# A four-layer transformer kernel on one core: room of its own for raw weights, a spread in four transfers, blocks of products of ones, and a new order

## What is computed

```python
x = x + 0.5 * L0_ffn(layernorm(x))      # gate, up, down; 704 hidden; weights (wq - 128) * scale; silu
x = x + L0_attn(layernorm(x))           # 16 heads of 16, causal, rope
x = x + 0.5 * L0_ffn(layernorm(x))
x = x + 0.5 * L1_ffn(layernorm(x))      # weights quantised to -1, 0, 1 by their mean magnitude, sigmoid
x = x + L1_attn(layernorm(x))           # 16 query heads on 4 key heads, causal, alibi, output bias
x = x + 0.5 * L1_ffn(layernorm(x))
```

## Time and profile before

| what | value |
|---|---|
| median of three runs | 583.99 us (583.89 to 584.03) |
| span of the profiled execution | 584.2 us |
| busy in that span | PE 535.6, DVE 461.8, ACT 401.5, POOL 340.4 us |
| mean granted clock of TensorE | 0.984 of full |

### The profile page before, as it was taken

The page is one execution under the profiler, slowest core; times in us unless marked ns, Lnnn a source line. Parts: engine busy times, 40 slices in busy tenths (PEclk is TensorE's granted clock), DMA queues, the critical chain, the costliest instruction groups (busy, mean ns, idle before and its releaser), DMA issues.

```text
span 584.2 us, 12653 instructions
## 1 busy us (share of the span) xinstructions
PE 535.6 (92%) x4924; PEld 290.7 (50%) x4924; DVE 461.8 (79%) x813; ACT 401.5 (69%) x605; POOL 340.4 (58%) x427
## 2 busy tenths in 40 slices
PE   2887987998999999999899998999999999999987
PEld 1353642544653654655546564465455644553664
DVE  4888979898889789589986878887897767783454
ACT  5866576678577758855687756867769596669433
POOL 2367886864896578844645167624455724437543
PEclk9978997999999999999999999999999999999999
DMA  8700020121022100310210102010211021001301
GB/s 327 311 2 1 22 88 1 55 74 42 20 85 65 37 4 3 121 65 1 77 40 3 47 17 74 22 41 0 69 41 38 4 78 50 22 1 41 111 0 73
DMA packets 19627, 31.73 MB, mean 54 GB/s; under 512 B 6464, under 2 KB 7872, under 8 KB 19416
## 3 DMA queue, kind: packets, MB, share of 16 engines
q1 hardware_dynamic: 19568, 30.93, 15.0%
HBM read 13.75 MB, written 2.36 MB: 28 GB/s over the span
## 4 chain that ended last, share of the span: by engine, by line
PE 57%; DVE 14%; ACT 9%; POOL 7%; issue 7%; DMA 5%; SPq 1%; DVEq 0%; POOLq 0%; ACTq 0%
PE PS L583 17%; PE PS L607 10%; PE PS L694 9%; PE PS L674 4%; DVE MX L1050 4%; PE PS L625 4%; PE PS L659 4%; PE PS L567 3%; ACT PB L838 3%; PE PS L709 3%; DMA RB<-scratch 2%; ACT XN L761 2%; PE PS L539 1%; DVE MX L1046 1%; DVE ST L863 1%
## 5 line engine op out<-in xcount | busy, mean ns | idle before, releaser
L838 ACT ACTIVATE PB<-PS 128x1024 f32<-128x1024 f32 x160 | 158.9, 1024 | 50.3 <-PE PS L674 43.2
L1050 DVE TENSOR_REDUCE MX<-PS 128x2 f16<-128x1024 f32 (+2 forms) x192 | 158.4, 865 | 23.1 <-PE PS L539 22.9
L583 PE MATMUL PS<-XT,WGU 128*128 128x512 f16 x660 | 158.2, 382 | 2.8 <-DVE PB L990 1.1
L1126 POOL TENSOR_TENSOR HH<-TH,HH 128x512 f16<-128x512 f32 x71 | 82.2, 1168 | 86.1 <-ACT HH L806 85.8
L1154 POOL TENSOR_SCALAR_AFFINE_SELECT PB<-PB 128x512 f32<-128x512 f32 (+1 forms) x140 | 73.2, 550 | 53.1 <-ACT PB L838 53.1
L583 PEld LDWEIGHTS PS<-XT,WGU 128*128 128x128 f16 x660 | 59.1, 98 | 74.1 <-issue 5.9
L607 PE MATMUL PS<-WD,HH 128*128 128x256 f16 x660 | 78.0, 273 | 1.1 <-POOL HH L1126 0.6
L694 PE MATMUL PS<-PB,V 128*32 128x512 f32 (+3 forms) x1024 | 75.5, 435 | 1.3 <-POOL PB L1154 1.1
L607 PEld LDWEIGHTS PS<-WD,HH 128*128 128x128 f16 x660 | 62.4, 98 | 14.0 <-issue 3.1
L659 PE MATMUL PS<-SK,SQ 63*128 63x256 f16 (+3 forms) x512 | 60.7, 300 | 6.5 <-DVE MX L1050 3.6
L674 PE MATMUL PS<-SQ,SK 64*128 64x384 f16 (+3 forms) x512 | 58.5, 300 | 8.0 <-ACT PB L838 2.4
(11 more groups left out here) (122 smaller groups left out, 756.4 us busy)
## 6 DMA issues: line engine op xcount, KB each, us to landing
SQ<-QPB SPq DMA_DIRECT2D x24, 256.0 KB, 2.5
OC<-OT SPq DMA_DIRECT2D x16, 256.0 KB, 2.4
RB<-scratch SPq DMA_DIRECT2D x32, 128.0 KB
SK<-QPB SPq DMA_DIRECT2D x12, 256.0 KB, 3.1
SQ<-MT SPq DMA_DIRECT2D x128, 1.0 KB
out<-X SPq DMA_DIRECT2D x8, 256.0 KB, 2.2
PB<-gu SPq DMA_DIRECT2D x2, 704.0 KB, 6.1
X<-x_in SPq DMA_DIRECT2D x2, 512.0 KB, 5.4
```

The lines of the kernel that those rows point to most:

```text
L583: m = e.matmul(o[:, :], WGU[l][:, k, col:col + P], rows_of(f)[j][:, k, :], start=j == 0 and k == 0, stop=j == 1 and k == 1)
L838: e.activation(PB[Q % 2][:, j, :, :], two_banks("s", i), ACT.Exp, scale=0.25).then_inc(a_exp, 1)
L1050: e.tensor_reduce(mx[:, :, pr, t], o[:, :, col:col + (t + 1) * P], AX.X, ALU.max, negate=True).then_inc(a_max, 1)
L1126: e.tensor_tensor(hh[1][:, s * T:(s + 1) * T], value_of(j)[0], hh[0][:, s * T:(s + 1) * T], ALU.subtract).then_inc(f_lo, 1)
```

## The change

Raw weights get a tile of their own, `LATE`, and ACT's late `k` letters wait for nothing but the masks' semaphore. `R` issues four transfers, one for each group of 32 neighbouring partitions, each with 16 as its outermost number of repeats; the semaphore rises by 64. A new PE letter `z` runs eight products of ones (128x128 by 256 columns, 16 bits) into a PSUM bank that nobody reads, after a wait for `ONE`. The new string has 17 of them: ten ahead of the first `t`, then one, two, two, one and one, all before the first `m`. The batches' rows, rotation table and masks are loaded ahead of the raw weights of layer 1. POOL sets its three constants first. All strings and banks are written anew; apart from `z`, each engine has the same letters as before, the same number of each. The scratch room for software transfers is set to 256 bytes; the kernel has no such transfer.

```diff
 ORDER = {
     "sp":
-        "kkrrkrkrDSrRDSRrkrDSRkrrDSRrrDrkSRkDSRrrlkkrDrSRrDSlRrkrkDrSRrDSrRrkkrDrSRDrSRrDkrkSRDrSRrrrDSRDOSOR"
-        "OOOOOO",
+        "kkrkrrkDrSrRDSRrrkDSkRrrDSRrrDrkSlRkDSRrrkkrrDSRrlDSRrkkrrDSrDRSrRrkkrDSrDrSRRrDrkkSRDrSRrOOrrDSRDSR"
+        "OOOOOO",
     "pe":
-        "ttggGggGaGgttGGggGggddddGaGgtggGuutGqqddddvqgGgvgqGGGgugugGqttqmmgmgmmmmmqmsqsdsmgGmsdmsdmmsdsmmpmsG"
+        "zzzzzzzzzzttzgggGGgGGggttzzaGggggGdddgdzzGGtatzgGGuuqqqddddvqgggggGGGGvuugGttqqzmmmggmmmmmqmsqssdmgG"
...
     "dve":
-        "NwNtthwwhwkhwhwhtwthwwNhhwwdwNdwhnhwhkuuhtpqptqdwdpqhnpqhhkuuhhhpqttqpmmmmmxmmmspqsmhpmqxhmdmsmmdmxm"
+        "NwNtthNhhkhwwwttwhhwwhhwwdNdwwwnhhwwhuukphptwqqdtppdhnqqhhhhkuuhttpqpqmmmmmmxmmssmqqpphmxhmdmmmsmxmd"
...
     "act":
-        "TwwXxxwttthXtthxxhhwhtwhkttwwwthwhXtkhwxthYwyyhthXxkQQvtkthQtvYQtyytthhxxhhQTkQkktthkeeeteeQeeQhhoee"
+        "TwwXxxwtwthkttXtthxxhhkkhhtttkwwwhthXktXYyyxhhxthhvQQttthkttwYvyQyQtxxhhhhwThkktQQteweeewteeQeQhhoee"
...
     "pool":
-        "wrwwrhhhhwhwrdhdrewhhhhsasqdadsqaesaqqhwshsahahqqhfsafsdfafqdhqfffffhefhffcfhCffhcCssaaqqfffrssadaqq"
+        "wwwrrrhhhhhdhdrewwhhhhssadaqqdsesaaqqhssaawhhhhqqssfaafwfdqfqdffhhfefffffhcfffhhCcCssaaqfffrsqadsaqq"
...
-ONE_BANK, TWO_BANKS, SHARED = "tgGuqvoapd", "ms", "do"
+ONE_BANK, TWO_BANKS, SHARED = "tgGuqvoapdz", "ms", "do"
...
+        LATE = sb("LATE", [P, 2, 4 * T])
...
-        late = [t[1][:, :, :].rearrange("p h t -> p (h t)").bitcast(F32) for t in (SQ, SK)]
+        late = [LATE[:, k, :] for k in range(2)]
...
+        ONES = ONE.bitcast(BF16)
...
             e.dma_start(BO[:, :], bo1).then_inc(l_a0, 16)
+            e.dma_start(X[:, 2 * NT:, :], x_in[:, 2 * NT:, :]).then_inc(l_x23, 16)
+            e.dma_start(ROPE[:, :, :], rope).then_inc(l_c2, 16)
+            e.dma_start(MASKW[:, :, :, :], maskw).then_inc(l_c2, 16)
+            e.dma_start(MASKM[:, :, :, :], maskm).then_inc(l_c2, 16)
             e.dma_start(rd[0], wd1[:, 0:4, :]).then_inc(l_w3, 16)
             e.dma_start(rd[1], wd1[:, 4:, :]).then_inc(l_w3, 16)
             for k in range(2):
                 e.dma_start(rgu[k], gu1[:, k, :]).then_inc(l_w1, 16)
-            e.dma_start(X[:, 2 * NT:, :], x_in[:, 2 * NT:, :]).then_inc(l_x23, 16)
-            e.dma_start(ROPE[:, :, :], rope).then_inc(l_c2, 16)
-            e.dma_start(MASKW[:, :, :, :], maskw).then_inc(l_c2, 16)
-            e.dma_start(MASKM[:, :, :, :], maskm).then_inc(l_c2, 16)
...
-                    w.wait_ge(t_si[u], 32 * (n - 1))
+                    w.wait_ge(t_si[u], 64 * (n - 1))
...
-                    for g in range(2):
-                        e.dma_start(RB[g:P:2, u, :], src[:, g, :].unsqueeze(1).to_broadcast([4, 16, T])).then_inc(t_si[u], 16)
+                    for a in range(4):
+                        e.dma_start(RB[32 * a:32 * a + 32, u, :], src[a].unsqueeze(0).to_broadcast([16, 2, T])).then_inc(t_si[u], 16)
...
-                if c == "a":
+                if c == "z":
+                    w.wait_ge(p_pool, 3)
+                    wait_bank(w, "z", i)
+                    o = bank("z", i)
+                    for _ in range(8):
+                        e.matmul(o[:, 0:256], ONES[:, 0:P], ONES, start=True, stop=True)
+                elif c == "a":
...
                     w.wait_ge(l_c2, 48)
-                    if z == 1:
-                        w.wait_ge(p_dve, 30)
...
-                    w.wait_ge(t_si[u], 32 * (n + 1))
+                    w.wait_ge(t_si[u], 64 * (n + 1))
...
-    nc = bacc.Bacc("TRN2", target_bir_lowering=False, num_devices=1)
+    nc = bacc.Bacc("TRN2", target_bir_lowering=False, num_devices=1, dynamic_dma_scratch_size=256)
```

More of the change, by code:

```diff
@@ new lines @@
+        "smdsmmdsmdsmmpmssGmsgsGmsspmssgmmGmmpsmsmsgssGmmmpmssvsvmsmsuummmpqqssoooomssddsqqmmmpttdsssdgmsggsG"
+        "GggmpmmsGsmssmmgsGGmmpssmmvvuussddmmddsmqqspmottosoossgsmqgmggmGGGsgmspsmmgssGqtGtpssgdsssdddpggGgGm"
+        "mgvgmmmvGuuGGmmooomoqmsqmssqmsmdsmddmdmssmmspmsmssmmsttspgssmgGGgggmmsGGgGmsspmsttddddssmggpmmmvgggu"
+        "uGsGGssqmqsmgGsmqGssoompmmddddmssomsommpmttsssggssGGsgmmmpsgGmssgmmGGgmpsmsvsmsmmmdddmsdsspssmttoomm"
+        "gggsGuuooqqqGsmmsgmGGsggGsmpmmsdmmsddsmsdmsspsmsmsmmspttvsmmggggGGGGggGsmmssttssddddoooommpsmpuugsmm"
@@ new lines @@
+        "qqssqsggsGGssspmsmgGmmpmmvgmmmGgmssGsmststmmpddddssmoomgssoomsggmGGmsmpmsgsssGggssspssttGGpggGgddddG"
+        "GgggGGooooddddttgGggGgGgGGgdddd",
+    "dve":
+        "NwNtthNhhkhwwwttwhhwwhhwwdNdwwwnhhwwhuukphptwqqdtppdhnqqhhhhkuuhttpqpqmmmmmmxmmssmqqpphmxhmdmmmsmxmd"
+        "mkhmsnmhmxmsmmhmmmcsxhmmmmcmmuxummmppxqqooNdmqppmmmqttdcmsxhsshhnkmsmmmhmmxsshhmmmmxcuudmmdNppmqqmtt"
+        "ooNmxmhpmhqkhmhmmxhqptthcsdhdknsshchmssmmmmhuuxshmmhoommlmlxmmmdlmdmmxNmmmmmxttNmhhkchmmhhhmmxttddnm"
+        "shsmmmskcsuuhxhhmlmssmlhhlommxmddmNmmmoxmttNhhmmchkmmhmxhmhmmmcxmmmmddnmxttmmosssuuhokhlllhmmmshssxh"
+        "hmmmmcmdxmdmNmmmmNxttmmchhkhhhhmmttddxnoomNmmuuhmmxlllckhhmmhmmmxmmmmmchhmxmttdmdmomhxoNmmhhmmmxkhch"
+        "httchhddhkhhhooNXttddhhhkhhhdd",
@@ new lines @@
+    "act":
+        "TwwXxxwtwthkttXtthxxhhkkhhtttkwwwhthXktXYyyxhhxthhvQQttthkttwYvyQyQtxxhhhhwThkktQQteweeewteeQeQhhoee"
+        "eteheeoeetYoeeeteehhhoeeevveeyycceoeeQeeQXoxxQeeeQtetthehhtoeeeettheYhhoevevcyyeeceeXoxxeQeetettXQhh"
+        "ehtteeoheetxxQhheoeeeetQhottthhtvtYvcyyhchheQQeeeQeeeeoeeXexxeeoteethhtttheXthhheeoxxeeettYcovhttyye"
+        "heeQhhteteQcQeehheeeoXoxxeeetteeethhoetheetXthhhoeeveeceeecoeexxYttteyyhQQQeehhtetthehhoeeeeeeoeeeXe"
+        "oxxvettXhththhttheeheexxcceYeooyytXeQQeeeQthteeeeohhetovttheeeeehhoxxcceeteeetthXhehoeeeteteeeeetoxx"
+        "hhhotctthhhtctthhhXxxttthhhtthhth",
@@ L139 @@
+        "frffhffhhhhccCCeffhhfhhhfffddfffrrhhchchhffCCbefrfffffhfhbhhhccCCffrfhhffffffhhchChchChhhrhhhhh",
     "banks":
[L140 to L143, removed]
@@ L144 @@
[L144 to L146 removed]
+        "3722733416563147324563743511241352071653540260761313765406145146726450134763462014242642612652402606"
+        "2560260426046250426050264205624064025264026520650304620126401624716240210426153204612476201652702640"
@@ new lines @@
+        "6206246102642046324602740246012564216026502470636201624604621460362530467204257024520764620572351624"
+        "5620436402460364704206205604206247620740264563206423416420643212064213460253472506720526027520430624"
+        "3641264024660360246054027647240725426056241043046304620461244272406730462705431043604261470246724162"
+        "4146202642460620462065401264137543601370246032640167420641245026452064270456024602546056024260456205"
+        "62046520727204740621463206720462416420672046043210607521503274167416342731672414571",
```

20 lines of the change are left out of this document (1 added, 19 removed).

## The result

| kernel | median | runs | against before |
|---|---|---|---|
| before | 583.94 us | 582.37 to 584.03 (4) | |
| after | 575.83 us | 573.70 to 576.52 (4) | 0.9855 [0.9835, 0.9875] |

The change is 8.1 us faster, where I had forecast 3.0 (581.0; the range 575.5 to 585.5 holds it). Its profiled execution has a span of 574.1 us and a mean granted clock of 0.988, beside 584.2 and 0.984 before. The two profiles are not quite a fair pair. Of the 10.1 us between the two spans some 2 belong to that one execution. A line number of the changed kernel lies eight to ten above that of the same statement before.

What follows compares the result with a forecast made beforehand. DVE was taken to bound the first 101.7 us, with PE busy for nearly all the rest. Terms of -1.0, -0.5, -0.5 and -1.0 summed to -3.0 us: forecast 581.0 us, range 575.5 to 585.5.

Steps and rivals of the forecast that it cites:

- E: Spread in four transfers: each lands 1.5 us sooner; -1.0 us in all, range -2.0 to +1.1.
- B: First 40 us in the new order: PE gains a lead but DVE bounds the stage; -1.0 us, between -3.3 and +1.7.
- D: Own room for raw weights: ACT's last four fills no longer wait for quantising; -0.5 us, range 0 to -2.1.
- A: Ten blocks ahead of the first rows: end at 13.8 us, first unit 1.3 us late but at 2.4 GHz.
- C: Seven other blocks: hidden by PE's wait for DVE, returning lower-clock time; -0.5 us taken.
- F: New order past 101.7 us: 19.6 us of holes can shrink or grow, -2 to +2; 0 taken.
- rival "slower": Ahead of the first turns: blocks overrun, ending at up to 19.8 us; price up to 5, 586 us; chance 0.15.
- fewer than three stretches at the lower level: Sign for PE's clock: lower-level stretches number fewer than three after 16 us.
- a DMA share well above 0.25: Sign for the spread: RB's transfers show this share and POOL's waits are shorter by 1.5 us each.
- rival "nothing": PE's lead waits for DVE and PE's other work hides the spread: 583.0 to 585.0 us; chance 0.12.
- check on row maxima: Sign at the first stage's end: row maxima from about 86 us instead of 88.2.
- check on idle time past 101.7: Sign that the forecast is wrong: idle time past 101.7 us over 21 us.

Runs made afterwards that it cites:

- e8: Kernel before with four transfers for a spread and nothing else new: 582.10 us, 0.9962.
- e7: New strings without blocks of ones up to the first row maxima, old strings behind, with the change's loads and room: 580.74 us, 0.9934.
- e3: Changed kernel with new strings, blocks included, up to the first row maxima and the old strings from there on: 583.45 us, 0.9993.
- e10: Changed kernel whose strings switch to the old ones at the end of the third attention, about 260 us: 581.23 us, 0.9954.
- e13: Changed kernel with old strings only from the first row maxima to 260 us, new front with 17 blocks and new order behind: 578.79 us, 0.9900.
- e5: Changed kernel without the ten blocks of ones ahead of the first rows, the other seven kept: 572.10 us, 0.9787.
- e6: Changed kernel with the ten blocks ahead of the first rows and none of the other seven: 572.01 us, 0.9791.
- e2: Changed kernel without any of its 17 blocks of ones, orders and banks else unchanged: 571.86 us, 0.981.
- e14: Changed kernel with POOL's two late w letters moved early and the first ten blocks alone: 571.01 us, 0.9776.
- e12: Changed kernel with POOL's two late w letters moved early and no blocks of ones: 570.84 us, 0.9774.
- e11: Changed kernel, all blocks kept, with POOL's two late w letters moved ahead of its first d: 568.86 us, 0.974.
- e15: Changed kernel with POOL's two late w letters moved early and the seven later blocks alone: 567.22 us, 0.9703.
- e9: Changed kernel with all strings old and no blocks; own room, new load order and four transfers kept: 586.33 us, 1.0034.
- e1: Changed kernel with the spread put back to two transfers, all else new: 576.15 us, 0.9868.

## Why the prediction was right and wrong

The direction and the range were right. The size was not: of the terms in my sum of -3.0 one was far off, and the others were wrong in ways that partly cancelled. Each row below is the difference of two kernels' medians, in an order in which the change can be built up from before.

| term | forecast | measured | from |
|---|---|---|---|
| E, the spread | -1.0 | -2.1 | e8 against before |
| B and D: loads, room, order of the front | -1.5 | -1.4 | e7 against e8 |
| A and C, blocks | -0.5 | +2.7 | e3 against e7 |
| F, order past the first row maxima | 0 | -7.6 | after against e3 |
| sum | -3.0 | -8.4 | after against before: -8.1 |

The 0.3 between the last two numbers is that between the medians of before beside e8 and beside the changed kernel (584.24 and 583.94).

**F is the step that failed.** I argued that the strings have the same letters and stand within two steps of each other at each attention's end, that 19.6 us of holes could shrink or grow by 2, and took 0. The new order was worth 7.6 us. The strings also stand further apart between those ends: of PE's 651 steps behind the cut 313 have moved, 276 of them by one or two places and 37 by three to eight. The holes past 101.7 were not the ceiling either: against e3, 2.3 of the 8.7 us were time in which PE counted as busy. The waits of PE's weight loads past 100 us show what closed (us in total, times, longest us). The kernel before:

```profile
PEld PS L674 <- ACT PB L838: 9.9, 22, 1.0
PEld PS L659 <- ACT PB L838: 6.3, 17, 0.8
PEld PS L674 <- DVE MX L1050: 6.3, 15, 0.8
PEld PS L659 <- DVE MX L1050: 3.8, 10, 0.7
PEld PS L583 <- ACT PB L838: 3.2, 8, 0.7
```

The changed kernel:

```profile
PEld PS L684 <- ACT PB L846: 6.5, 16, 1.1
PEld PS L669 <- ACT PB L846: 6.4, 15, 0.8
...
PEld PS L684 <- DVE MX L1058: 4.7, 12, 0.6
PEld PS L669 <- DVE MX L1058: 2.8, 7, 1.0
...
PEld PS L593 <- ACT PB L846: 1.8, 5, 0.6
```

Scores and maxima wait less for banks that exponentials (`PB`) and row maxima (`MX`) still hold: in these rows the waits for `PB` fall from 9.9 to 6.5 and from 3.2 to 1.8 (one group stays, 6.3 and 6.4), those for `MX` from 10.1 to 7.5. All such waits of weight loads together are 22.1 and 14.6 us before, 21.6 and 15.8 in e3, and 16.7 and 11.7 in the changed kernel: they stay with the old order and fall with the new. e10 and e13 show that the gain is gathered all along. One such wait lasts about 0.4 us on the mean (6.5 us in 16 times) and at most 1.1, and there are dozens, so exchanges that give PE other work meanwhile add up; my bound of 2 us for 651 letters of PE rested on no row. Which exchanges carry it was not tried, nor was the new order with the old assignment of banks, or the reverse; I had put the bank tables at nothing too. So it is shown that the order behind the cut, with its banks, carries the gain; that it does so through the shorter waits is argued from these rows.

**A was right in kind and too careful.** The ten blocks ended at 12.5, not 13.8; the turns began at 12.37, the first `h` at 16.30, not 17.9, as the clock rose after 3.2 us and not 5.4. The rival "slower", blocks that overrun, did not happen. Yet the ten blocks brought nothing that the medians show (e5 and e6 against e2, e14 against e12): PE was made faster in a stage that DVE bounds, as step B said.

**B took DVE for the bound, rightly, and then missed what a faster PE sets off on it.** I had costed DVE's steps at their durations in the trace of before, without asking which POOL steps would run beside them in the new strings. The sign was there to read. DVE's and POOL's timelines of the kernel before:

```profile
52.63 1.35 DVE L1001 TENSOR_TENSOR PB<-TH,PB 64x512 f16<-64x512 f32 x1
```

```profile
51.09 2.35 POOL L1090 TENSOR_TENSOR WA<-PB,WA 128x768 f16<-128x768 f32 x1
```

The DVE step began while POOL's ran, and took 1.35 us; in the changed kernel the same step lasts 0.68 at 56.92. After the change both late `w` letters of POOL stand against one `w` of DVE, 7.5 us for 2.8. e11 shows the price with the blocks in place: 7.0 us; without them it is 1.0 to 2.1 (e2 against e12), since PE's slow products then hold DVE up instead. ACT's first fill of a stack, at 31.99 us before, stands earlier in the new string, and there ACT waits 2.15 us for the masks, a wait that I had not listed:

```profile
20.77 1.06 ACT L753 ACTIVATE SQ<-ROPE 128x1024 f32<-128x1024 f32 x1 [2.15 <-DMA MASKM<-maskm]
```

**C costed the seven blocks at nothing for PE and -0.5 for the clock.** It held only where POOL is out of the way: there the seven bring 4 us (e15 against e12), with a clock of 1.00 instead of 0.80 from 45 to 62 us. In the change itself the seventeen cost 4.0 us (e2), and 2.5 of these are there by the first transpose of maxima (94.83 against 92.35), where POOL's steps hold up DVE's `w` for 7.5 us against 6.6. My check "fewer than three stretches at the lower level" came out (about 53.2 to 60.0 and 94.1 to 97.5), but the first lasted 6.8 us, where the stretch at the same place had 3.3 before. Why each group alone is free in the change, and both together are not, stays open: the profiles show DVE's 7.5 us with the seven alone too, and in e5 the first transpose of maxima starts at 94.61, just 0.2 us ahead of the changed kernel, though e5 is 3.7 us faster; so the front alone does not explain the cost. The runs of the changed kernel and of e2 spread over 2.8 and 3.8 us, so part of those 4 us may be scatter; e3 and e7, which spread over 1.4 and 1.0, leave 2.7 of them without that doubt.

**B and D together came out at -1.4 for -1.5 by luck.** D has no run of its own. With the old strings, loads and room together cost 4.2 us (e9 against e8), and the new strings of the front then give 5.6 back (e7 against e9). Neither number is a term of my sum.

**E had its mechanism right and its size half.** I took 3.8 us from the first issue to the last landing, 1.5 us less than before. Where POOL stood waiting and SP issued the four without a break, POOL's step starts 4.25 us after the first issue (251.74 to 255.99), where before it was mostly 5.1 to 5.5; four issues stand 0.62 us apart and not 0.57, and each lands 2.3 us later and not 2.0. So about 1 us was saved there. Three other spreads of the changed kernel for which POOL waited took 4.8 to 5.7 us from first issue to POOL's step. In the old order the saving took two of POOL's seven waits and 2.1 us of the time (e8), twice what I forecast. In the new order it is 0.3 (e1); I take it that the end of those stages is set elsewhere there, but no run shows it. Behind e11 it is 2.0 to 2.5 again, with intervals that overlap. The check "a DMA share well above 0.25" came out, with 0.62 and 0.73. (The Trainium skill, DMA: Bandwidth & Descriptors, section "Why a DMA increments its semaphore by 16 and not by 1", has the outermost sizes of the two sides decide on the number of engines, here 4 or 16; the shares, 0.25 before and up to 0.73 after, agree.)

The rival "nothing" rested on a misread row: in the windows of the earlier trace rows PE is busy for 87% and 95%, together 91%, not 95%.

The check on row maxima (86 us forecast, 87.91 measured) missed and named its cause: the front had no lead left. The check on idle time past 101.7, "over 21 us", was set against a loss and had no counterpart for a gain: PE's idle time past 100 fell to 17.0 us.

## What to carry to other kernels

Where an order is written by hand, an exchange of two steps behind the bound is a term of its own: bound it by all waits that it could shorten (how often PE waits for a bank that a slow reader holds), and not by a round number. Before making one engine faster, list which steps of POOL will then run beside DVE's; a long POOL step belongs where DVE is not reading the large tiles, and moving two letters there was worth 7.0 us with the blocks in place and 1 to 2 without them. Work that only keeps PE's clock up paid here where a hole of PE would follow and DVE was not held up (4 us), and showed no gain ahead of the first rows, in a stage that DVE bounds. Prices of such changes do not add: each was found only with the others in place.

## What the runs showed that I had not expected

- A DVE step of 0.585 us stood for 3.43 us beside one POOL step of 3.46 us; DVE's second kind of step went from 0.94 to 1.83 us each beside POOL's `WO` and `h`. In e11, with POOL elsewhere, the same steps take 0.58 and 0.95 again.
- POOL pays as well: its step for `WA` took 3.12 us alone and 3.46 beside DVE, and two steps `h` took 3.44 beside DVE, where one alone takes 1.16.
- After a dense start PE reached 2.4 GHz 3.2 us after its first product; with the mixed start of before it took 5.4.
- The granted clock's column reads 1.00 from the start, while durations show 1.2 GHz for PE's first 3.2 us of work in the changed kernel and 5.4 before: read durations there.
